# Weighing a part of layer one's edges on GpSimd in a graph attention kernel, with a new table of priorities

## The reference: what is computed

```python
# layer one: dot-product attention over the neighbours
q = x.reshape(n, 8, 32) * 32 ** -0.5;  k, v from inputs
scores = where(adj > 0, q @ k.T, -9e15); out = softmax(scores) @ v
x = layernorm(x + out)
# layer two: additive attention over the neighbours
h = x @ W.T + b;  e = leaky_relu(s_src[j] + s_dst[i], 0.2)
e = where(adj == 0, -1e9, e);  h2 = softmax(e) @ h
x = layernorm(x + elu(h2))
```

## Time and profile before

| | |
|---|---|
| median of 3 runs | 368.3 us (366.85 to 370.05) |
| the profiled execution | 371.5 us, its span 369.9 us |
| mean granted clock of TensorE | 0.786 of full speed |
| VectorE busy | 285.7 us (77%) |
| TensorE busy | 236.4 us (64%) |
| GpSimd busy | 211.9 us (57%) |
| ScalarE busy | 171.4 us (46%) |

### The profile page before, as it was taken

One profiled execution on the slowest core, in us unless ns is written; L12 is line 12 of the kernel. 1 busy time (PEld: TensorE's weight loads), 2 busy tenths in 40 slices (PEclk: granted clock), 3 DMA queues, 4 the chain that ended last, 5 costly groups with the idle time before them and its releaser, 6 DMA issues. The chain is left out here.

```text
span 369.9 us, 5119 instructions
## 1 busy us (share of the span) xinstructions
PE 236.4 (64%) x1238; PEld 165.5 (45%) x1238; DVE 285.7 (77%) x834; ACT 171.4 (46%) x466; POOL 211.9 (57%) x327
## 2 busy tenths in 40 slices
PE   0374758464796586778869687892443974487780
PEld 0262536232474464446547354551322752275550
DVE  2976798799989999889999879697415386687783
ACT  4532376457244466644763444610020059166555
POOL 8472464453872477667527771327777777777300
PEclk9998596765688699869969899955585788598695
DMA  7977166468487356866107552014444454646301
GB/s 286 396 230 207 40 245 219 129 231 283 153 303 268 141 162 171 297 219 186 48 17 205 144 142 61 33 46 101 118 114 105 110 131 128 155 110 169 96 0 63
DMA packets 24513, 57.91 MB, mean 157 GB/s; under 512 B 6592, under 2 KB 14912, under 8 KB 22432
## 3 DMA queue, kind: packets, MB, share of 16 engines
q0 software_dynamic: 10032, 31.77, 31.0%
q1 hardware_dynamic: 14448, 25.77, 19.7%
HBM read 53.20 MB, written 4.33 MB: 156 GB/s over the span
## 5 line engine op out<-in xcount | busy, mean ns | idle before, releaser
L1087 POOL DMA_INDIRECT e_ring<-in_kv,e_col_i x78 | 76.1, 975 | 36.6 <-issue 22.3
L1087 POOL DMA_INDIRECT e_ring<-table,e_col_i x78 | 75.4, 967 | 25.2 <-issue 22.4
L1458 PE MATMUL e_po<-e_weighted,e_sel_edges 128*128 128x264 f32 x158 | 44.6, 421 | 3.1 <-DVE e_weighted L1740 3.1
L1180 ACT ACTIVATE e_search<-e_search 128x2048 bf16<-128x2048 int32 x16 | 39.8, 2487 | 9.2 <-issue 4.0
L1536 DVE MAX8 e_raw<-e_search 128x8 f32<-128x512 f32 (+2 forms) x56 | 38.6, 722 | 4.2 <-ACT e_search L1180 3.6
L1405 PE MATMUL e_pq<-e_left,e_sel_rows 128*128 128x256 bf16 x156 | 38.9, 348 | 0.0
L1458 PEld LDWEIGHTS e_po<-e_weighted,e_sel_edges 128*128 128x128 f32 x158 | 31.2, 207 | 9.9 <-DVE e_weighted L1740 4.6
L1666 DVE TENSOR_TENSOR e_prod<-e_pq,e_ring 128x512 f32<-128x512 f32 (+1 forms) x40 | 26.0, 673 | 10.6 <-DMA e_ring<-in_kv,e_col_i 6.9
L1740 DVE TENSOR_TENSOR e_weighted<-e_ring,e_pc 128x528 f32<-128x528 f32 (+1 forms) x42 | 27.0, 678 | 3.8 <-PE e_pc L1432 1.8
L1405 PE MATMUL e_pq<-e_xres,e_sel_rows 128*128 128x256 bf16 x78 | 26.9, 345 | 4.5 <-DVE e_prod L1666 4.5
L1458 PE MATMUL e_po<-e_left,e_search 128*128 128x264 f32 x84 | 27.9, 494 | 2.5 <-DVE e_left L1740 2.5
(11 more groups left out here) (228 smaller groups left out, 588.8 us busy)
## 6 DMA issues: line engine op xcount, KB each, us to landing
e_search<-in_adj SPq DMA_DIRECT2D x16, 1024.0 KB, 5.1
table<-e_hx SPq DMA_DIRECT2D x16, 136.0 KB, 3.3
e_ring<-in_kv SPq DMA_DIRECT2D x1, 2112.0 KB, 13.2
out<-e_prod SPq DMA_DIRECT2D x16, 128.0 KB, 2.2
e_ring<-in_kv,e_col_i POOLq DMA_INDIRECT x78, 4.1
e_ring<-table,e_col_i POOLq DMA_INDIRECT x78, 2.9
e_xres<-in_x SPq DMA_DIRECT2D x2, 512.0 KB, 7.3
e_xres<-in_x SPq DMA_DIRECT2D x3, 256.0 KB, 6.4
```

The costliest lines, as they stand in the source:

```text
L1087: nc.gpsimd.indirect_dma_start(out=rings[layer][:, q % RING[layer], :], out_offset=None, in_=kv if layer == 0 else table, in_offset=bass.I ...
L1180: nc.scalar.activation(val_signs[:, k % 2, :], adj_tile[:, k % 2, :], ACT.Sign, accum_out=signs[:, k:k + 1]).then_inc(s("sgn_ready"), 1)
L1458: last = nc.tensor.matmul(po[n % 2][:, 0:CV], selection(layer, q, 1)[:, 0, :], weighted[plan.weighed_into(b)][:, j * CV:(j + 1) * CV], sta ...
```

## The change

In layer one, the third, sixth, ... batch of each group but the last (`aside`) is weighed by GpSimd and no longer by VectorE. GpSimd can't read the weights in PSUM, so once a group VectorE copies them into a new tile `e_weights_0` (`copy_weights`). The copy waits for the group's weights and for GpSimd's last batch of the group before; GpSimd's stage `weigh_aside` waits for the copy, for its gathered rows and for the sums of the batch that had its buffer. A second semaphore, `weighed_aside`, counts these batches, and every wait on a weighed batch goes to the semaphore of the engine that weighed it. The table `LATER` is replaced as a whole.

```diff
--- before.py
+++ after.py
@@ -62,8 +62,8 @@
 V_FIRST = 15
 
 
-LATER = {"rows": 2.0, "sign": 20.0, "norm": 0.5, ("gather", 0): 2.0, ("weigh", 0): -20.0, ("sums", 0): 2.0, ("turn", 0): 1.0, ("fill", 0): 5.0,
-         "turn_pens": 0.5, "evac": 20.0, ("back", 1): 0.5, "elu": 1.0, "emit": 2.0}
+LATER = {"rows": 5.0, ("sums", 0): 20.0, "spread_of": -20.0, "turn_src": 20.0, "flags": 5.0, "turn_pens": -20.0, "count": -3.0,
+         "far": 20.0, "emit": 20.0, "elu": 2.0, ("diagonal", 0): 5.0}
 
 
 class Steps:
@@ -115,6 +115,7 @@
                     c += m
                 self.batches[layer, g] = pairs
         self.batch0[2, 0] = len(self.reports)
+        self.where = [(layer, g, i) for layer in range(2) for g in range(len(GROUPS)) for i in range(len(self.batches[layer, g]))]
         self.pieces = {}
         i = 0
         for g in range(len(GROUPS)):
@@ -152,6 +153,15 @@
         n0 = self.batch0[1, 0]
         return b % WEIGHTED[0] if b < n0 else (b - n0) % WEIGHTED[1]
 
+    def aside(self, b):
+
+        layer, g, i = self.where[b]
+        return layer == 0 and g < len(GROUPS) - 1 and i % 3 == 2
+
+    def weighed_by(self, b):
+
+        return sum(self.aside(i) == self.aside(b) for i in range(b + 1))
+
     def place_before(self, b):
 
         return max([i for i in range(b) if self.weighed_into(i) == self.weighed_into(b)], default=None)
@@ -269,6 +279,16 @@
 
     def piece(i):
         return [p for g in range(NG) for p in plan.pieces[g] if p[1] == i][0]
+
+    def weighed(b):
+        return ("weigh_aside" if plan.aside(b) else "weigh",) + where[b]
+
+    def all_weighed(b):
+
+        return [weighed(max(i for i in range(b) if plan.aside(i) == x)) for x in (False, True) if any(plan.aside(i) == x for i in range(b))]
+
+    def last_aside(g):
+        return weighed(max(i for i in range(plan.batch0[0, g + 1]) if plan.aside(i))) if g >= 0 else None
 
     def listed(q):
         g = plan.group_of_q(q)
@@ -323,18 +343,17 @@
 
     def gather_stages(layer, g):
         for q in range(plan.q0[g], plan.q0[g] + plan.C[g]):
-            after = [("weigh",) + where[plan.batch_of[layer, q - RING[layer]]]] if q >= RING[layer] else []
+            after = [weighed(plan.batch_of[layer, q - RING[layer]])] if q >= RING[layer] else []
             if layer == 0:
                 after += [listed(q), ("mean_v", 3) if q >= V_FIRST else None]
             else:
-                after += [("store", NK - 1), ("weigh",) + where[len(where) // 2 - 1], ("back", 1, plan.behind(q) - 1) if plan.behind(q) else None]
+                after += [("store", NK - 1), *all_weighed(len(where) // 2), ("back", 1, plan.behind(q) - 1) if plan.behind(q) else None]
             put("POOL", 1.25, 100 * layer + g, ("gather", layer, q), *after, lag=2.5)
 
     def edge_stages(layer, g):
         n, rank = layer * NG + g, 100 * layer + g
         early = rank - (1.3 if layer else 0.3)
         b0, nb = plan.batch0[layer, g], len(plan.batches[layer, g])
-        last = ("weigh",) + where[b0 + nb - 1]
         if layer == 0:
             m, k0 = len(GROUPS[g]), plan.k0[g]
             put("POOL", 0.6 * m, rank - 0.5, ("left_1", g), ("x", g), ("queries", g - 2, len(plan.batches[0, g - 2]) - 1) if g >= 2 else None)
@@ -355,21 +374,26 @@
             before = ("sums",) + where[plan.batch_of[0, q + m - 1 - TURNED]] if q + m > TURNED else None
             put("ACT", 0.13 * m + 0.1, rank + 0.5, ("copy_edges", q, m), ("turn_edges", q, m), before, frees="pt")
         one_before = bank_before(plan, n)
-        put("PE", 0.7, early, ("turn", layer, g), scores, one_before and ("weigh",) + where[one_before - 1], listed(NQ - 1) if n == NG - 1 else None)
+        put("PE", 0.7, early, ("turn", layer, g), scores, *all_weighed(one_before), listed(NQ - 1) if n == NG - 1 else None)
         put("DVE", 2.0 if g == BIG_GROUP else 1.4, early, ("scan", layer, g), ("turn", layer, g), last_pens("copy_pens", g), ("exp",) + divmod(n - 1, NG) if n else None)
         put("ACT", 0.35, early, ("exp", layer, g), ("scan", layer, g), ("back",) + divmod(n - 1, NG) if n else None)
         put("PE", 0.5, early, ("back", layer, g), ("exp", layer, g))
         for i, (c0, m) in enumerate(plan.batches[layer, g]):
             b = b0 + i
             had = plan.place_before(b)
-            put("DVE", 0.34 * m, rank - 0.1, ("weigh", layer, g, i), ("back", layer, g), ("sums",) + where[plan.reporting(had)] if had is not None else None)
+            if layer == 0 and i == 0 and plan.aside(b0 + 2):
+                put("DVE", 0.25, rank - 25, ("copy_weights", g), ("back", 0, g), last_aside(g - 1))
+            if plan.aside(b):
+                put("POOL", 0.62 * m, rank - 0.1, ("weigh_aside", layer, g, i), ("copy_weights", g), ("sums",) + where[plan.reporting(had)] if had is not None else None)
+            else:
+                put("DVE", 0.34 * m, rank - 0.1, ("weigh", layer, g, i), ("back", layer, g), ("sums",) + where[plan.reporting(had)] if had is not None else None)
             firsts = [plan.k0[g] + j for j, t in enumerate(GROUPS[g]) if c0 <= plan.c_first[t] < c0 + m]
             for k in firsts:
                 before = layer * NK + k - 2
                 put("ACT", 0.3, rank - 0.5, ("diagonal", layer, k), ("filled", g), (("norm" if before < NK + 1 else "norm_a"), (before - 1) % NK) if before >= 1 else None)
                 free = ("norm" if before < NK else "norm_a", before % NK) if before >= 0 else None
                 put("PE", 0.6, rank - 0.2, ("fill", layer, k), ("diagonal", layer, k), ("copy_mean", layer), free)
-            put("PE", 0.62 * m, rank - 0.1, ("sums", layer, g, i), ("weigh", layer, g, i), turned(layer, plan.q0[g] + c0 + m - 1), *[("fill", layer, k) for k in firsts])
+            put("PE", 0.62 * m, rank - 0.1, ("sums", layer, g, i), weighed(b), turned(layer, plan.q0[g] + c0 + m - 1), *[("fill", layer, k) for k in firsts])
 
     def tile_stages(layer, k, rank):
         end = last_sums(layer, k)
@@ -870,6 +894,7 @@
         weighted_0 = sb("e_weighted", [P, WEIGHTED[0], 2 * CV])
         left_flat = left[:].rearrange("p a b k c -> p (a b k c)")
         weighted = [weighted_0[:, i, :] for i in range(WEIGHTED[0])] + [left_flat[:, C + i * 2 * CV:C + (i + 1) * 2 * CV] for i in range(WEIGHTED[1] - WEIGHTED[0])]
+        weights_0 = sb("e_weights_0", [P, P])
         rden = sb("e_rden", [P, H])
         y = sb("e_y", [P, 4, C])
         below_zero = left[:, 0, 0, 0, :]
@@ -947,6 +972,15 @@
         def at_least(eng, name, n):
             if n > 0:
                 eng.wait_ge(s(name), n)
+
+        def weighed_all(eng, b):
+            for x in (False, True):
+                some = [i for i in range(b) if plan.aside(i) == x]
+                if some:
+                    weighed_one(eng, some[-1])
+
+        def weighed_one(eng, b):
+            eng.wait_ge(s("weighed_aside" if plan.aside(b) else "weighted_ready"), plan.weighed_by(b))
 
         def lens(g):
             return len(GROUPS[g]), plan.k0[g], plan.q0[g], plan.C[g]
@@ -1073,7 +1107,7 @@
                 if stage[0] == "gather":
                     _, layer, q = stage
                     if q >= RING[layer]:
-                        pool.wait_ge(s("weighted_ready"), plan.batch_of[layer, q - RING[layer]] + 1)
+                        weighed_one(pool, plan.batch_of[layer, q - RING[layer]])
                     if layer == 0:
                         pool.wait_ge(s("found"), plan.found_by(q))
                         if q >= V_FIRST:
@@ -1081,7 +1115,7 @@
                     elif q == 0:
                         for i in range(2):
                             pool.wait_ge(table_stored[i], 16 * (NT // 2))
-                        pool.wait_ge(s("weighted_ready"), plan.batch0[1, 0])
+                        weighed_all(pool, plan.batch0[1, 0])
                     if layer and plan.behind(q) > plan.behind(q - 1):
                         pool.wait_ge(s("weight_turned"), NG + plan.behind(q))
                     nc.gpsimd.indirect_dma_start(out=rings[layer][:, q % RING[layer], :], out_offset=None, in_=kv if layer == 0 else table,
@@ -1157,6 +1191,19 @@
                     own.did(nc.gpsimd.tensor_scalar(bad[:, 2, :], found_n[:], 0.0, 0.0, ALU.is_equal, ALU.is_equal))
                     own.wait()
                     nc.gpsimd.tensor_scalar(bad[:, 1, :], end[:], 0.0, None, ALU.is_gt).then_inc(s("bad_ready"), 1)
+                elif stage[0] == "weigh_aside":
+                    _, _, g, i = stage
+                    b = plan.batch0[0, g] + i
+                    c0, m = plan.batches[0, g][i]
+                    at = (plan.q0[g] + c0) % RING[0]
+                    pool.wait_ge(s("weights_copied"), g + 1)
+                    for j in range(m):
+                        arrived(pool, 0, plan.q0[g] + c0 + j)
+                    had = plan.place_before(b)
+                    if had is not None:
+                        pool.wait_ge(s("sums_done"), plan.reports_by(had))
```

(13 more changed lines are left out.)

## The result

The changed kernel took **372.57 us** (median of 4 executions, 372.48 to 374.73) where the kernel before took 368.19 in the same session (366.85 to 370.05): ratio 1.0105 with a 95% interval of 1.0053 to 1.0157, slower by 1%. In another session with the same level of times it was 372.87 against 368.92, ratio 1.0089 (1.0058 to 1.0120). The forecast was 364.2, so the sign was wrong; the time lies inside the range of 356.5 to 374.

The account below looks back on a forecast made before the run. VectorE was taken to bound layer one, GpSimd's gathers layer two. The terms -6.7 + 1.5 + 1.5 - 0.4 = -4.1 us took 368.3 to 364.2 us, range 356.5 to 374.

Parts of the forecast that it names:

- The weighing: Layer one: VectorE loses ten weighings, nine of two chunks and one of one, 6.7 us less work.
- The copies: Layer one: six copies of weights from PSUM on VectorE, 0.25 us each, cost 1.5 us; their wait nothing.
- GpSimd's price: Layer one: ten weighings on GpSimd take 10.5 us, for which it has room.
- The lock: Layer one: VectorE stalls on the SBUF ports shared with GpSimd cost 1.5 us, ends 0 and 10.5.
- Everything blocked: Rival: all of VectorE is blocked beside GpSimd's weighing, +5.3 us, 373.6 us; chance 0.05.
- The order: End of layer one: new priorities put the last tile's spread first, winning 0.4 us; bounds 8.1 won to 8 lost.
- the relief is not on the path: Rival, layer one: VectorE is freed but other engines set the chains, or the order loses the gain; 368 us, chance 0.18.
- The move as a whole: Layer one: weighing, copies and lock together, without the order, win 3.7 us.
- forecast mark: Sign expected: layer two's first gather at about 243 instead of 247.2 us, layer two and tail unchanged.
- the likeliest case: Whole kernel: the forecast itself, 364.2 us, own range 360.5 to 367, chance 0.44.
- the signs of being wrong: First gather of layer two not earlier; layer one's six last gathers behind a GpSimd weighing; tail changed by over 1 us.
- GpSimd's queue and the last gathers: Rival, end of layer one: group five's GpSimd weighings delay the last group's gathers; 370.5 or 376.4 us, chance 0.18.

Follow-up runs that it names:

- e9: Changed kernel with the old priority table, so the move to GpSimd alone, against the kernel before: 368.88 us, ratio 0.9987, lower level.
- e12: Move with the old table, two of every three batches on GpSimd instead of one, against the kernel before: 371.09 us, ratio 1.0037.
- e10: The changed kernel, unmodified, run again beside e9, against the kernel before: 372.87 us, ratio 1.0089, lower level.
- e18: Move with the old table without its entry (weigh, 0), against the kernel before: 367.64 us, ratio 0.9949, lower level.
- e4: Changed kernel with no weighing on GpSimd in group five, against the kernel before: 409.24 us, ratio 1.0030, upper level.
- e17: Changed kernel with the table entry (weigh, 0) back at -20, against the kernel before: 378.91 us, ratio 1.0251, lower level.
- e7: Move with the old table but rows at 5 instead of 2, against the kernel before: 410.52 us, ratio 1.0119, upper level.
- e11: Changed kernel with the table entry (turn, 0) back at 1, against the kernel before: 381.32 us, ratio 1.0311, lower level.
- e16: Move with the old table but (sums, 0) at 20 instead of 2, against the kernel before: 405.01 us, ratio 0.9891, upper level.
- e3: The changed kernel, unmodified, run again, against the kernel before: 403.93 us, ratio 0.9924, upper level.
- e15: The kernel before, unmodified, run again for one more trace: 410.63 us, upper level.

## Why the prediction was wrong, by its steps

**The weighing, -6.7 us: right.** The forms of 528 and 264 elements took 50.3 + 1.7 us before and 44.5 + 1.3 after, 6.2 less, and the same in e9 within 0.2.

**The copies, +1.5 us: right.** Six of 0.244 us by the median. Their place at the head of the queue cost 0.8 us of waiting in all in the changed kernel.

**GpSimd's price, 10.5 us: right.** 9 x 1.082 + 0.627 = 10.4.

**The lock, +1.5 us: the size of it depends on the order.** With the move alone VectorE's busy time went from 285.7 to 283.0 us, 2.7 less where weighings and copies make it 4.7 less (-6.2 + 1.5): 2.0 us of stalls. In the changed kernel it went to 279.3, 6.4 less: 1.7 us of the old stalls are gone too. The addition of x in layer one took 1.97 us at most in e9, 1.06 after and 1.33 before. Which instruction is hit is seen in e9, at 49 us beside GpSimd's subtractions and at 130 us beside one of the new weighings. GpSimd:

```profile
49.14 1.89 POOL L1129 TENSOR_TENSOR e_left<-e_xres 128x1024 f32<-128x1024 f32 x1 [1.33 <-DMA e_xres<-in_x]
51.11 1.95 POOL L1134 TENSOR_TENSOR e_left<-e_left 128x1024 f32<-128x1024 f32 x1
...
57.90 1.09 POOL L1205 TENSOR_TENSOR e_weighted<-e_ring,e_weights 128x528 f32<-128x528 f32 x1
...
131.09 1.08 POOL L1205 TENSOR_TENSOR e_weighted<-e_ring,e_weights 128x528 f32<-128x528 f32 x1
```

VectorE beside it:

```profile
49.15 2.16 DVE L1694 SCALAR_TENSOR_TENSOR e_hit<-e_slot_e,e_rel 128x256 f32<-128x256 f32 x1
...
51.24 1.22 DVE L1583 MAX8 e_raw<-e_search 128x8 f32<-128x1024 f32 x1
...
57.35 1.31 DVE L1794 TENSOR_TENSOR e_weighted<-e_ring,e_pc 128x528 f32<-128x528 f32 x2
...
130.50 1.97 DVE L1543 SCALAR_TENSOR_TENSOR e_y<-e_y,e_xres 128x256 f32<-128x256 f32 x1
```

The list step with two SBUF operands takes 2.16 us beside GpSimd, where its kind takes 0.485; the search with one (1.22) and the two weighings that read PSUM (1.31 together) are not touched. The addition of x, two SBUF operands again, takes 1.97 us where its kind takes 0.426, and ends only behind GpSimd's weighing. In e12 a list step at 57.84 us takes 2.35 beside two weighings on GpSimd of 2.11 together. In the changed kernel no addition of x or list step was held up for long beside a weighing; its two longest additions (0.96 and 1.06) stand beside GpSimd's subtractions. The rule that the prediction took from the Trainium skill ("SBUF — State Buffer", "Who interferes with whom") is what this trace shows. "Everything blocked" fell.

**The order, -0.4 us: this is the step that failed, and it carried the sign.** It measured +4.0 us at the lower level (e10 against e9), and 6 to 7 read off at an equal clock. The spread that I priced is not even earlier: after, the diagonals start at 238.5 us, still ahead of the norm's step at 239.1. What the order did instead stands earlier in layer one: VectorE's idle time before layer two is 10.6 us greater than with the old order (46.1 against 35.5 in e9), most of it before score products, whose waits are 12.8 us against 2.8. Which entries do it stays open. The text said that the order can't be read from the diff, set bounds of 8.1 won to 8 lost, and then took a value next to nothing from the one move that a row could price. The bounds held; the value had no better claim than any other between them. The rival "the relief is not on the path" named the possibility (the order loses what the unloading won) and stopped it at 370.

**The move as a whole, -3.7 us: seen in the traces, not in the medians.** e9 shows the forecast mark, the first gather at 243.3 (forecast 243), and layer two and tail unchanged (121.6 us against 122.7). But that trace is of a short execution and the one of before of a long one. By the medians it is 368.88 against 368.92, nothing, and 1.7 us with e18's table; at an equal clock about 2 to 2.5 us are there. So the relief was counted in full and came in part. In the session of e9 and e10 the sum missed by 8.1 us (-4.1 forecast, +4.0 measured): 4.4 of them are the order's and 3.7 the move's. Whether the move itself lowers the clock, and so eats its own gain, is open.

**Luck.** That the time fell inside the range of 356.5 to 374 owes nothing to the likeliest case, whose own range ended at 367. Of the signs of being wrong the first came true: the first gather of layer two is not earlier (249.3 against 247.2 us), though VectorE has less to do.

**GpSimd's queue and the last gathers:** one weighing does stand among them (220.0 us, 1.07 long), behind the fourth of the six, and VectorE waits 1.8 us for a later gather. e4, without it, is no faster, so it does not decide.

## What to carry to other kernels

A change that sets a planner's priorities anew has no small unknown: every engine's queue is written afresh, and here a single entry cost 1.6 to 2.2% (e17, e7, e11) or nothing (e16, e18). Give the order a wide, two-sided term that is not centred on zero by habit, and measure the change of work and the change of order apart, since the old order may suit the new work better than the one that came with it, and the two need not add. To read which it was, split the bound engine's time up to the next fixed point into busy and idle, and compare executions at a like clock.

## What the runs showed of the hardware

**Sessions of two levels.** The kernel before took 368 to 369 us in some sessions and 408 to 411 in others, in each of its 4 to 29 executions there (366.6 to 372.6 and 402.3 to 419.1 us; no execution lies between). It is not the chip: the chip numbered 6 gave 368.9 and then 410.5, the one numbered 8 gave 408.1 and then 369.3. At the upper level VectorE sits before some instructions that nothing in the profile releases ("remote"), mostly in layer two: from its first gather to the end of the span the changed kernel takes 149.7 us in e3 and 121.6 at the lower level. From e15, with the wait in brackets:

```profile
320.52 0.21 DVE L1503 RECIPROCAL e_rden<-e_po 128x8 f32<-128x8 f32 x1 [13.84 <-remote]
```

Four such waits before `e_rden` are 30.4 us in that trace; there were none in any trace of the lower level. In the one shown, TensorE's last sums before it had ended at 306.2 us, 14 us earlier. What holds it I can't say. The ratios differ between the levels by close to 2% (changed kernel 1.009 and 0.992), so a verdict from one level does not hold for the other.

**The clock.** Within one kernel and session, executions differ by 6 us, and the mean granted TensorE clock goes with it: 0.779 in a 372.5 us execution of before, 0.807 in a 368.6 us one. Which of the two is the cause is not shown. A trace of each kernel is not enough to size a gain of 3 us.
